# A residual stack of four conditioned layers on one core: feature order in SBUF, DMA shapes and the order of the loading phase

## The chip, the cores and the metric

The kernel runs on one core of one Trainium2 chip. The metric is the device time of one launch in microseconds (us).

## The reference

Four layers, each added to its input x (32 sequences of 128 steps with 512 features): a modulated linear layer, a tanh recurrence, a low-rank layer whose factors come from a small network on the condition, and an LSTM.

```python
x = x + (x * ys) @ weight * rsqrt((ys * ys) @ (weight * weight) + 1e-8)   # ys = cond / sqrt(512)
h = tanh(h @ Wh + x @ Wx + b);  x = x + all h                             # h starts from cond
ae = layernorm(cond) * ln_g + ln_b
xw = gelu(ae @ w1 + b1) @ w2 + b2            # w2: 512 x 8192, xw split into x_a, x_b (512 x 8 each)
x = x + (x + x @ (base + x_a x_b^T))
x = x + LSTM(x; Wx, Wh, b), h0 = cond, c0 = 0     # gates i, f, o, g of 512
```

## The kernel before

All data lie features by tokens: 512 features are 128 partitions times KC = 4 chunks. Work runs in 32 tiles of 4 time steps times 32 sequences (128 columns). Every weight matrix is split into two fp16 parts, high (on ACT, `high`, L477) and low (on DVE, `low`, L756), after its scale is known, and three of the four products of parts are summed on PE.

In the kernel before, feature 4p + c lies in partition p, chunk c. `by_row` loads a square weight that way with four rows, one run of 8 KB, per partition (L350). A tile of x (L354), cond (L613), the bias b1 (L375) and an output tile (L412) are moved with four DMAs each, in runs of 512 B, 128 B and 4 B (x and outputs 512 B, cond 128 B, b1 4 B). On PE a block of 128 output features is every fourth column of a weight (`columns`). The LSTM's gate weights (wx3, wh3) are laid out on the host by chunk and then by gate, and each matmul of `gates_x` (L1378) and `gates_h` (L1386) reads 512 columns in one run; four of them, for four strips of 32 array columns, run at a time.

**The loading phase.** Each engine's order is written out by hand. SP issues the loads in a fixed order: w0, x tile 0, wx1, wh1, w1, four 1 MB blocks of w2 into a ring of four slots (L360), x tiles 1 to 3, b1, wx3 (4 MB), w2 blocks 4 to 7, wh3 (4 MB, into slots freed by w0, wx1 and wh1), base, w2 blocks 8 to 15, b3 (L401), x tiles 4 and 5. Block n of w2 waits until PE's `w2_unit(n - 4)` has used the slot (`w2_used`). ACT issues cond and the layer norm's rows; DVE waits for these four DMAs together (`ld_rows`, 64) before the layer norm (L1070 to L1082), whose output starts PE's work (L1413). Between that and `gates_x(0)` PE runs two or three tiles of the first layers (`l0`, `l1`, `rnn`), 16 units of w2 (L1288), `turn_a`, `z(0)`, `x3_base(0)`, and after the last unit `move_b` (L1309) and `x3_low_rank(0)`. ACT takes squares of each weight for its scale (L480), makes the high parts and the recurrence's tanh (L592); DVE makes the low parts and sums; POOL spreads maxima over partitions (L430). `gates_x(0)` needs x3, so the b factors: `b_magnitude(3)`, `b_scale`, `b_high`, `b_low`, `x3_low_rank(0)`, `low_rank_share(0)`, `x3(0)` (L1001), `x3_high(0)` and the low part of x3.

**The loop** has 30 rounds of four LSTM steps, with a tile of the earlier layers between them, and ends with eight LSTM steps alone (two tiles of output).

## Time and profile before

| | us |
|---|---|
| median of 3 runs | 1192.1 (1191.29 to 1196.86) |
| the profiled execution | 1191.93 |
| its span, first to last instruction | 1190.1 |
| gates_x(0) starts, in the span | 107.16 |
| first lstm step starts | 114.86 |
| last output DMA is issued | 1187.6 |

The span is what the views below cut up; 1.83 us lie outside it. PE is busy for 95% of it.

### The profile page before, as it was taken

What the parts mean: (1) busy time and instruction counts of PE and PEld (TensorE: products, weight loads), DVE (VectorE), ACT (ScalarE), POOL (GpSimd) and SP (SyncE); (2) the same over time, 40 slices, a digit from 0 to 9 for tenths busy, and PEclk for the clock granted to TensorE, in tenths of its full rate; (3) what the DMA queues carried; (4) which work ended last, traced back from release to release, by engine and by line L of the source; (5) the groups of instructions that cost most, each with busy time, mean ns of one, the idle gap of its engine ahead of it and who ended that gap; (6) DMA issues with size and microseconds to landing.
All of it is one profiled execution on the core that took longest, in us unless ns stands there. A gap on an engine that the chain in (4) does not pass through costs nothing.

```text
span 1190.1 us, 50661 instructions
## 1 busy us (share of the span) xinstructions
PE 1133.2 (95%) x22740; PEld 756.6 (64%) x22740; DVE 911.4 (77%) x2645; ACT 425.3 (36%) x1032; POOL 56.2 (5%) x75
## 2 busy tenths in 40 slices
PE   2886999999999999999999999999999999999896
PEld 1653676667666766676677667766776677667542
DVE  4896777787777787877877778777787787777665
ACT  4794333333333332333333323333333233333221
POOL 1000000000000000000000000000000000000000
PEclk9987999999999999999999999999999999999998
DMA  9991000000000000000000000000000000000000
GB/s 323 388 347 42 3 21 20 21 20 21 20 13 10 21 21 21 20 21 20 12 12 21 20 20 21 21 21 11 13 20 21 20 21 21 11 10 5 12 11 19
DMA packets 49065, 51.00 MB, mean 43 GB/s; under 512 B 5984, under 2 KB 38752, under 8 KB 47184
## 3 DMA queue, kind: packets, MB, share of 16 engines
q1 hardware_dynamic: 47984, 47.50, 12.8%
q8 instruction: 178, 2.92, 1.0%
q10 hardware_dynamic: 864, 0.26, 0.1%
q14 instruction: 39, 0.32, 0.1%
HBM read 39.36 MB, written 8.39 MB: 40 GB/s over the span
## 4 chain that ended last, share of the span: by engine, by line
PE 90%; DVE 4%; ACT 2%; DMA 2%; issue 1%; ACTq 0%; DVEq 0%
PE ps_gates L1386 28%; PE ps_gates L1378 27%; PE ps_l L1317 14%; PE ps_x L1317 7%; PE ps_rnn L1402 6%; PE ps_rnn L1405 4%; PE ps_z L1317 2%; PE ps_lr L1317 2%; DMA ring<-in_hw 1%; PE ps_gates L1288 1%; DVE big L756 1%; DMA hb1T_sb<-in_hb1T 1%; ACT wh_hi L477 0%; DVE gates_ring L1012 0%; DVE late L1031 0%
## 5 line engine op out<-in xcount | busy, mean ns | idle before, releaser
L1386 PE MATMUL ps_gates<-big,lstm_h 128*32 128x512 f16 x6144 | 354.4, 379 | 4.4 <-DVE lstm_h L1034 4.4
L1378 PE MATMUL ps_gates<-big,rows 128*32 128x512 f16 x6144 | 345.8, 381 | 3.5 <-DVE rows L756 3.5
L1378 PEld LDWEIGHTS ps_gates<-big,rows 128*32 128x32 f16 x6144 | 165.3, 97 | 172.1 <-issue 6.6
L1386 PEld LDWEIGHTS ps_gates<-big,lstm_h 128*32 128x32 f16 x6144 | 158.1, 97 | 161.7 <-DVE lstm_h L1034 7.3
L599 ACT ACTIVATE gates_ring<-gates_ring 128x256 f32<-128x256 f32 x128 | 53.4, 418 | 337.9 <-DVE gates_ring L1012 337.9
L1012 DVE SCALAR_TENSOR_TENSOR gates_ring<-ps_gates,tile_un,rows 128x256 f32<-128x256 f32 x256 | 111.8, 477 | 68.3 <-PE ps_gates L1386 67.1
L1402 PE MATMUL ps_rnn<-rnn_h,wh_hi 128*128 128x64 f16 x2048 | 120.3, 192 | 6.9 <-DVE rnn_h L855 6.9
L1405 PE MATMUL ps_rnn<-rnn_h,wh_lo 128*128 128x32 f16 x2048 | 116.3, 177 | 0.0
L1402 PEld LDWEIGHTS ps_rnn<-rnn_h,wh_hi 128*128 128x128 f16 x2048 | 93.0, 96 | 35.3 <-issue 27.2
L1031 DVE SCALAR_TENSOR_TENSOR late<-gates_ring,tile_g,cell_tanh 128x128 f16<-128x128 f32 x128 | 45.0, 352 | 60.8 <-ACT cell_tanh L606 60.8
L1405 PEld LDWEIGHTS ps_rnn<-rnn_h,wh_lo 128*128 128x128 f16 x2048 | 91.2, 97 | 0.0
L1317 PE MATMUL ps_l<-xs,w_hi 128*128 128x128 f16 x1024 | 79.7, 222 | 2.1 <-DVE xs L756 1.9
L1317 PE MATMUL ps_l<-x,wx_hi 128*128 128x128 f16 x1024 | 79.3, 221 | 0.4 <-DVE x L756 0.4
L1317 PE MATMUL ps_x<-x,base_hi 128*128 128x128 f16 x1024 | 78.3, 219 | 0.0
L1317 PEld LDWEIGHTS ps_l<-xs,w_hi 128*128 128x128 f16 x1024 | 65.0, 114 | 3.2 <-DVE xs L756 2.0
L1317 PEld LDWEIGHTS ps_l<-x,wx_hi 128*128 128x128 f16 x1024 | 64.7, 114 | 1.4 <-issue 0.8
L1317 PEld LDWEIGHTS ps_x<-x,base_hi 128*128 128x128 f16 x1024 | 63.8, 114 | 0.4 <-issue 0.4
L592 ACT ACTIVATE x_ring<-rnn_pre 128x128 f32<-128x128 f32 x128 | 39.6, 310 | 64.6 <-DVE rnn_pre L849 64.6
L1037 DVE STREAM_TRANSPOSE lstm_hT<-lstm_h 128x128 f32<-128x128 f32 x128 | 53.5, 418 | 4.4
L477 ACT ACTIVATE x<-x_ring,tile_s 128x512 f16<-128x512 f32 x32 | 23.1, 722 | 84.8 <-DVE x_ring L860 84.8
L477 ACT ACTIVATE rnn_h<-x_ring,scales 128x128 f16<-128x128 f32 x128 | 51.5, 402 | 4.2
L606 ACT ACTIVATE cell_tanh<-cell 128x128 f32<-128x128 f32 x128 | 39.8, 311 | 33.0 <-DVE cell L1022 33.0
(181 smaller groups left out, 1560.2 us busy)
## 6 DMA issues: line engine op xcount, KB each, us to landing
ring<-in_hw SPq DMA_DIRECT2D x16, 1024.0 KB, 13.4
xT_sb<-in_xT SPq DMA_DIRECT2D x128, 64.0 KB, 2.4
outT<-late SPq DMA_DIRECT2D x128, 64.0 KB, 2.1
big<-in_wx SPq DMA_DIRECT2D x5, 1024.0 KB, 7.9
big<-in_wh SPq DMA_DIRECT2D x5, 1024.0 KB, 13.4
big<-in_w SPq DMA_DIRECT2D x1, 1024.0 KB, 5.8
big<-in_hw SPq DMA_DIRECT2D x1, 1024.0 KB, 11.8
late<-in_base SPq DMA_DIRECT2D x1, 1024.0 KB, 19.5
```

The source lines that it names most:

```text
L477: return nc.scalar.activation(out_, in_, ACT.Copy, scale=scale)
L592: nc.scalar.activation(h, rnn_pre[:], ACT.Tanh).then_inc(rnn_h_ready, 1)
L599: nc.scalar.activation(gates[:, 0:2 * P], gates[:, 0:2 * P], ACT.Sigmoid).then_inc(gates_acted, 1)
L606: nc.scalar.activation(cell_tanh[:], cell[:], ACT.Tanh).then_inc(cell_tanh_ready, 1)
L1012: nc.vector.scalar_tensor_tensor(gates[:, half], ps_gates[t % 2][:, half], tile_un[:, a, 0:1], b3_sb[:, half], ALU.mult, ALU.add).then_inc ...
L1031: nc.vector.scalar_tensor_tensor(lstm_hs, gates[:, 2 * P:3 * P], tile_g[:, following, 1:2], cell_tanh[:], ALU.mult, ALU.mult).then_inc(lst ...
L1037: nc.vector.transpose(lstm_hT[:], columns(lstm_h[:])).then_inc(lstm_hT_ready, 1)
L1317: last = nc.tensor.matmul(psum, w, x, start=(n == 0), stop=(n == len(triples) - 1))
L1378: nc.tensor.matmul(ps_gates[t % 2][B * j:B * j + B, :], x16[:, part, k, at:at + B], wx3_part(w_part, k)[:, GW * j:GW * j + GW], start=(n = ...
L1386: last = nc.tensor.matmul(ps_gates[t % 2][B * j:B * j + B, :], lstm_h16[:, part, k], wh3_part(w_part, k)[:, GW * j:GW * j + GW], start=Fal ...
L1402: nc.tensor.matmul(ps_rnn[:, at:at + 2 * B], wh1_hi[:, k, P * oc:P * oc + P], rnn_h16[:, k].rearrange("p h b -> p (h b)"), start=(k == 0), ...
L1405: last = nc.tensor.matmul(ps_rnn[:, at:at + B], wh1_lo[:, k, P * oc:P * oc + P], rnn_h16[:, k, 0], start=False, stop=(k == KC - 1))
```

## The change

Feature 128k + p now lies in partition p, chunk k, for all tensors. A tile of x, an output tile, cond and b1 are one DMA each, with 2 KB, 2 KB, 512 B and 16 B per partition; square weights come in four runs of 2 KB per partition. On PE and DVE blocks of features are contiguous. The gate matmuls read their 512 columns as 16 runs of 32, and the gates lie in PSUM by gate, chunk and column; b3 is loaded in that order with 16 DMAs of 128 B runs. cond is SP's first load, the layer norm's rows are ACT's, and hb1 has a semaphore of its own. base is loaded ahead of wh3. `x3` is cut into `x3_first` and `x3_low`; `rnn` on ACT into `rnn_tanh` and `rnn_high`. The orders of all five engines up to the loop are written anew; the parts of them not shown move the same calls (squares, high and low parts, tanh steps) to other places. The loop's order is as before.

```diff
         def by_row(w):
-            return w.rearrange("(p k) n -> p k n", k=KC)
-
-
-        def by_block(x, j):
-            return x.rearrange("(f k) j n -> j f k n", k=KC)[j]
-
-        def columns(x):
-            return x.rearrange("p (q c) -> p c q", c=KC)
-
-
-        def loaded_columns(w, oc):
-            return w.rearrange("p (k q c) -> p k q c", k=KC, c=KC)[:, :, :, oc]
+            return w.rearrange("(k p) n -> p k n", k=KC)
+
+
+
+        def tile_columns(w, j):
+            return w.rearrange("p (k g j q) -> p j g k q", k=KC, g=GATES, q=B)[:, j]
+
+        def by_gate(x):
+            return x.rearrange("p (g k q) -> p g k q", g=GATES, q=B)
+
+        def by_chunk(x):
+            return x.rearrange("p (k q) -> p k q", q=B)
...
             def load_x(c):
-                for j in range(KC):
-                    sp.dma_start(xT_sb[c % XT_RING][FB * j:FB * j + FB].rearrange("p k t b -> p k (t b)"),
-                                 by_block(xT[c].rearrange("p j t b -> p j (t b)"), j)).then_inc(ld_x[c % XT_RING], 16)
+                sp.dma_start(xT_sb[c % XT_RING][:].rearrange("p k t b -> p (k t b)"),
+                             xT[c].rearrange("p j t b -> p (j t b)")).then_inc(ld_x[c % XT_RING], 16)
...
+            sp.dma_start(condT_sb[:], condT).then_inc(ld_cond, 16)
             load_weight(w0, W0_SLOT, ld_w0)
...
-            for j in range(KC):
-                sp.dma_start(b1T_sb[FB * j:FB * j + FB], b1T.rearrange("(f k) j -> j f k", k=KC)[j],
-                             allow_slow_non_contiguous=True).then_inc(ld_b1, 16)
+            sp.dma_start(b1T_sb[:], b1T).then_inc(ld_b1, 16)
...
             for n in range(RING, 2 * RING):
                 sp.wait_ge(w2_used, n - RING + 1)
                 load_w2(n)
+            sp.dma_start(late[:].rearrange("p (k n) -> p k n", k=KC), by_row(base)).then_inc(ld_base, 16)
...
-                sp.dma_start(b3_sb[B * j:B * j + B], b3[j].partition_broadcast(B)).then_inc(ld_b3, 16)
+                for g in range(GATES):
+                    sp.dma_start(by_gate(b3_sb[B * j:B * j + B])[:, g],
+                                 b3.rearrange("k (g j q) -> g j k q", g=GATES, q=B)[g, j].partition_broadcast(B)).then_inc(ld_b3, 16)
             sp.wait_ge(x1_ready, 1)
...
-                for j in range(KC):
-                    sp.dma_start(by_block(out[a].rearrange("p j t b -> p j (t b)"), j),
-                                 x3T[a % 2][FB * j:FB * j + FB].rearrange("p k t b -> p k (t b)"))\
-                      .then_inc(st_out[a % 2], 16)
+                sp.dma_start(out[a].rearrange("p j t b -> p (j t b)"),
+                             x3T[a % 2].rearrange("p k t b -> p (k t b)")).then_inc(st_out[a % 2], 16)
...
-            def wh1_low(oc):
-                dve.wait_ge(wh1_hi_ready, oc + 1)
-                low(wh1_lo[:, :, P * oc:P * oc + P], loaded_columns(big[:, WH1_SLOT], oc), s_wh1,
-                    wh1_hi[:, :, P * oc:P * oc + P]).then_inc(wh1_lo_ready, 1)
+            def wh1_low(k):
+                dve.wait_ge(wh1_hi_ready, k + 1)
+                low(wh1_lo[:, k], loaded(big[:, WH1_SLOT])[:, k], s_wh1, wh1_hi[:, k]).then_inc(wh1_lo_ready, 1)
...
-            for j in range(KC):
-                act.dma_start(condT_sb[FB * j:FB * j + FB], by_block(condT, j)).then_inc(ld_cond, 16)
             act.dma_start(ln_rows[:, 0], cond).then_inc(ld_rows, 16)
             act.dma_start(ln_rows[:, 1], ln_g.partition_broadcast(B)).then_inc(ld_rows, 16)
             act.dma_start(ln_rows[:, 2], ln_b.partition_broadcast(B)).then_inc(ld_rows, 16)
-            act.dma_start(hb1T_sb[:], hb1T).then_inc(ld_rows, 16)
-
+            act.dma_start(hb1T_sb[:], hb1T).then_inc(ld_hb1, 16)
+
+
+            act.wait_ge(consts_ready, 1)
+            nc.scalar.activation(unused[:], cell[:, 0:1], ACT.Sqrt)
+            act.wait_ge(ld_w0, 16)
+            squares(big[:, SQ_SLOT], big[:, W0_SLOT], 1)
             act.wait_ge(ln_var_ready, 1)
             nc.scalar.activation(ln_s[:, 1:2], ln_s[:, 0:1], ACT.Sqrt).then_inc(ln_root_ready, 1)
-            act.wait_ge(ld_w0, 16)
-            squares(big[:, SQ_SLOT], big[:, W0_SLOT], 1)
             act.wait_ge(ld_wx1, 16)
             unused_squares(big[:, WX1_SLOT], 2, 1)
+            act.wait_ge(dsum_parts, 1)
+            nc.scalar.activation(folded, ps_x3[:], ACT.Copy).then_inc(dsum_moved, 1)
+            w0_high(0)
             act.wait_ge(aeT_ps, 1)
             nc.scalar.activation(aeT, ps_z[:, 0:P].rearrange("p (k b) -> p k b", b=B), ACT.Copy).then_inc(aeT_ready, 1)
-            act.wait_ge(dsum_parts, 1)
-            nc.scalar.activation(folded, ps_x3[:], ACT.Copy).then_inc(dsum_moved, 1)
-            act.wait_ge(ld_wh1, 16)
-            unused_squares(big[:, WH1_SLOT], 3, 2)
-            w0_high(0)
             xs_high(0)
             w0_high(1)
+            wx1_high(0)
...
             wh3_high(1, 1)
+            copy_rows(3)
+            rnn_tanh(7)
+            b_high()
             wh3_high(2, 0)
-            copy_rows(3)
             wh3_high(2, 1)
+            low_rank_share(0)
+            x3_high(0)
             wh3_high(3, 0)
-
-            nc.scalar.activation(unused[:], s_h, ACT.Sigmoid)
-            b_high()
+            wh3_high(3, 1)
+            rnn_high(7)
...
-            dve.wait_ge(ld_rows, 64)
+            dve.wait_ge(ld_rows, 48)
             linked(nc.vector.bn_stats(stats, ln_rows[:, 0]))
             linked(nc.vector.bn_aggr(moments, stats))
             nc.vector.tensor_scalar(ln_s[:, 0:1], moments[:, 1:2], LN_EPS, None, ALU.add).then_inc(ln_var_ready, 1)
             x_magnitude(0, 0)
+            xs(0)
...
             b_magnitude(3)
-            wh3_low(2, 0)
+            wh3_low(1, 0)
             b_scale()
             x3_bound()
             gate_scales(0)
             b_low()
+            wh3_low(1, 1)
+            wh3_low(2, 0)
+            x3_first(0)
             wh3_low(2, 1)
-            dve.wait_ge(lstm_hi_ready, 1)
-            low(lstm_h16[:, 1], condT_sb[:], tile_g[:, 0, 1:2], lstm_h16[:, 0]).then_inc(lstm_lo_ready, 1)
+            x3_low(0)
             wh3_low(3, 0)
-            x3(0)
             wh3_low(3, 1)
             rnn_out(7)
             x2(1)
+            dve.wait_ge(lstm_hi_ready, 1)
+            low(lstm_h16[:, 1], condT_sb[:], tile_g[:, 0, 1:2], lstm_h16[:, 0]).then_inc(lstm_lo_ready, 1)
             x2_low(1)
...
-                            nc.tensor.matmul(ps_gates[t % 2][B * j:B * j + B, :], x16[:, part, k, at:at + B],
-                                             wx3_part(w_part, k)[:, GW * j:GW * j + GW], start=(n == 0 and k == 0), stop=False,
+                            nc.tensor.matmul(by_gate(ps_gates[t % 2][B * j:B * j + B, :]), x16[:, part, k, at:at + B],
+                                             tile_columns(wx3_part(w_part, k), j), start=(n == 0 and k == 0), stop=False,
                                              tile_position=(0, B * j))
...
             pe.wait_ge(folds_ready, 3)
-            pe.wait_ge(ae_ready, 1)
-            for k in range(KC):
-                last = nc.tensor.transpose(ps_z[:, B * k:B * k + B], columns(ae)[:, k], ident[0:B, 0:B])
-            last.then_inc(aeT_ps, 1)
             pe.wait_ge(ys_ready, 2)
             pe.wait_ge(sq_ready, 1)
             folded_parts(ps_x3, ysq, w0_sq).then_inc(dsum_parts, 1)
+            pe.wait_ge(ae_ready, 1)
+            for k in range(KC):
+                last = nc.tensor.transpose(ps_z[:, B * k:B * k + B], ae[:, P * k:P * k + P], ident[0:B, 0:B])
+            last.then_inc(aeT_ps, 1)
...
+            w2_unit(3)
             pe.wait_ge(wx1_lo_ready, 2)
             l1(0)
-            w2_unit(3)
+            l0(1)
             pe.wait_ge(wh1_lo_ready, KC)
             pe.wait_ge(h0_lo, 1)
             rnn(0)
-            l0(1)
+            w2_unit(4)
             rnn(1)
-            w2_unit(4)
             w2_unit(5)
+            w2_unit(6)
             rnn(2)
+            w2_unit(7)
             l1(1)
+            turn_a()
             rnn(3)
-            w2_unit(6)
-            w2_unit(7)
             l0(2)
-            turn_a()
             rnn(4)
-            rnn(5)
-            l1(2)
             w2_unit(8)
             w2_unit(9)
+            rnn(5)
             w2_unit(10)
-            w2_unit(11)
             pe.wait_ge(a_lo_ready, 4)
             z(0)
+            w2_unit(11)
+            l1(2)
             rnn(6)
+            w2_unit(12)
+            w2_unit(13)
+            rnn(7)
+            w2_unit(14)
+            w2_unit(15)
+            move_b()
             pe.wait_ge(base_lo_ready, 2)
             x3_base(0, range(KC))
-            w2_unit(12)
-            w2_unit(13)
-            w2_unit(14)
-            rnn(7)
-            w2_unit(15)
-            move_b()
             pe.wait_ge(b_lo_ready, 2)
```

## Rows read from the trace of the kernel before

**Rows 1.** Windows of the loading phase and of the loop: us, busy us per engine, PEclk, DMA, GB/s.
```profile
14.67:107.16 92.49, 66.48 (x852) 42.65 (x853) 78.55 (x186) 72.23 (x97) 8.31 (x12) 0.90 0.87 306
120.00:1130.00 1010.00, 1006.96 (x20820) 682.98 (x20821) 789.80 (x2329) 335.42 (x888) 47.05 (x56) 1.00 0.07 17
```

**Rows 2.** The chain of waits in order of time, from the start to 130 us: start us, us, what.
```profile
5.07 9.57 DMA hb1T_sb<-in_hb1T
...
18.43 0.69 DVE rows L1082
...
80.62 13.07 DMA ring<-in_hw
...
98.58 1.28 ACT L693
...
103.47 1.01 DVE big L756
...
104.67 0.75 DVE late L1001
...
106.26 0.77 DVE rows L756
...
107.16 7.88 PE ps_gates L1378 x96
...
118.59 0.71 PE ps_z L1317 x24
...
121.98 1.34 PE ps_x L1317 x24
...
126.89 5.18 PE ps_gates L1378 x96
```

**Rows 3.** Windows: the last two columns are the DMA engines' busy share and GB/s.
```profile
44.00:50.00 6.00, 4.12 (x79) 3.09 (x77) 3.56 (x12) 3.80 (x7) 0.00 (x0) 1.00 1.03 379
55.00:65.00 10.00, 10.00 (x186) 8.52 (x184) 9.79 (x15) 9.45 (x13) 0.00 (x0) 1.00 1.00 412
75.50:80.50 5.00, 5.00 (x51) 1.44 (x48) 4.60 (x15) 4.65 (x7) 0.32 (x1) 1.00 0.40 118
91.00:93.00 2.00, 0.66 (x25) 0.56 (x21) 1.27 (x3) 0.26 (x1) 0.00 (x0) 1.00 1.22 217
```

**Rows 4.** DMA view of 27 to 31 us: packets and bytes in it.
```profile
DMA packets 2166, 0.86 MB, mean 215 GB/s; under 512 B 747, under 2 KB 2146, under 8 KB 2150
```

**Rows 5.** Timeline of PE: start us, us, line, operation, tiles [idle before <-releaser].
```profile
64.96 0.28 PE L1402 MATMUL ps_rnn<-rnn_h,wh_hi 128*128 128x64 f16 x4
...
76.92 3.64 PE L1288 MATMUL ps_gates<-ring,lstm_h 128*32 128x512 f32 x32
...
89.63 1.07 PE L1288 MATMUL ps_gates<-ring,lstm_h 128*32 128x512 f32 x8 [1.86 <-DMA ring<-in_hw]
...
93.74 1.07 PE L1288 MATMUL ps_gates<-ring,lstm_h 128*32 128x512 f32 x8 [2.08 <-DMA ring<-in_hw]
95.52 3.46 PE L1309 MATMUL ps_l<-rows,half_ident 128*64 128x512 f32 x8 [0.72 <-ACT rows L543]
```

**Rows 6.** Timeline of SP: the issues of b3.
```profile
81.11 2.81 SPq L401 DMA_DIRECT2D rows<-in_b  x4
```

**Rows 7.** Timeline of ACT: its first activation.
```profile
15.76 0.20 ACT L620 ACTIVATE rows<-rows 32x1 f32<-32x1 f32 x1 [8.93 <-DVE rows L1072]
```

**Rows 8.** Low parts on DVE from 15 to 107 us, by line: busy us, mean ns.
```profile
L756 DVE SCALAR_TENSOR_TENSOR big<-big,l_scales 128x1024 f16<-128x1024 f32 x16 | 20.4, 1278 | 0.5 <-issue 0.3
L756 DVE SCALAR_TENSOR_TENSOR wh_lo<-big,scales,wh_hi 128x512 f16<-128x512 f32 x4 | 4.5, 1138 | 0.0
```

**Rows 9.** Timeline of the end: the last hidden state's transposition, the last tile's issue.
```profile
1184.12 0.31 DVE L1034 STREAM_TRANSPOSE lstm_h<-late 128x128 f16<-128x128 f16 x1
...
1185.73 2.50 SPq L412 DMA_DIRECT2D outT<-late  x4
```

**Rows 10.** The page, part 6: output DMAs, KB each, us from issue to landing.
```profile
outT<-late SPq DMA_DIRECT2D x128, 64.0 KB, 2.1
```

## Prediction before the run

> **What bounds the kernel now.** I read the windows first. In the loop PE is busy for 1006.96 of 1010 us at full clock [rows 1], so nothing there gets faster unless PE has less to do; the change leaves its instructions, their number and their sizes alone. What can give is the part outside: 107.16 us until `gates_x(0)` starts [rows 2], and the end.
>
> In the loading phase three things are near their limit. DVE is busy for 78.55 of 92.49 us, ACT for 72.23 [rows 1]. The DMA engines are at or above a busy share of 1.00 in most windows at 379 to 412 GB/s, but not from 75.5 to 80.5 us, where the share is 0.40 and the rate 118 [rows 3]. The chain of waits says which ends last. It starts with hb1T's landing at 14.64 (5.07 + 9.57), although the layer norm needs nothing of hb1; it crosses the long wait for a w2 block (issued at 80.62, 13.07 us), and from the last block runs through the b factors to `gates_x(0)` [rows 2]. So the question is when the last w2 block lands, now 93.74 us, and what follows it, now 107.16 - 93.74 = 13.42 us [rows 2, 5].
>
> The stretch without DMA work has its cause on PE: units 8 to 11 of w2 run at 76.92, 3.64 us for 32 matmuls, behind `rnn(5)` and `l1(2)` [rows 5]. Their ring slots come free only then, and everything loaded earlier has run out.
>
> **The change part by part.** Sums are made against the profiled execution, 1191.93 us, which is 0.17 below the median of the runs. The times of the loading phase are in the span.
>
> *Small packets.* From 27 to 31 us, when x tiles 1 to 3 and b1 are moved, 2166 packets carry 0.86 MB at 215 GB/s [rows 4]: 4 us x 16 engines / 2166 = 29.5 ns for one, and 91 to 93 us, with x tiles alone, run at the same 217 [rows 3]. Before, three tiles are 3 x 512 packets of 512 B and b1 512 of 4 B: 2048 x 29.5 ns / 16 = 3.8 us. After, the tiles go in 2 KB like w2, 0.79 MB at 379 GB/s = 2.1 us, and b1 is 128 packets, 0.2 us: 1.5 us less. x tile 0 and cond were 1024 packets, 1.9 us; now 0.26 MB at 379 and 128 packets, 0.9: 1.0 less. Together -2.5 us.
>
> The Trainium skill (DMA: Bandwidth & Descriptors, "Specifications") has 512 B as the smallest transfer that reaches line rate. The rows disagree: 512 B pieces ran at 217 against 379 for 2 KB. By the rule the x tiles would give nothing; that is rival C.
>
> *Larger pieces lost.* Five square weights of 1 MB go from 8 KB to 2 KB runs. wh3 and base, in 8 KB, ran at 412, w2 in 2 KB at 379 [rows 3]; 5.24 MB x (1/379 - 1/412) = 1.1 us at most, and none at least, since the other loads share those windows. I take +0.5.
>
> *The stretch without work.* In the new order units 8 and 9 come right after `rnn(4)`, unit 10 after `rnn(5)`, unit 11 after `z(0)`. Each slot then is refilled as its block has landed and been used, with two or three blocks still queued. Filling it gives 5 us x (1 - 118/395) = 3.5 us, at a rate midway between 379 and 412. This holds only if PE reaches unit 8 before the queue runs dry, so if `rnn(4)` is done by about 68 us. It should be: the layer norm waits for three DMAs that are issued 2.8 us earlier (cond's four issues are gone from ACT) and not for hb1, so `ae`, at 19.12 now (18.43 + 0.69 [rows 2]), comes about 5 us earlier; and ACT, idle for 8.93 us until 15.76 behind the layer norm's root [rows 7], takes w0's squares as soon as w0 is there. With 5 to 6 us of lead all through, `rnn(4)` (64.96 now [rows 5]) falls near 60. DVE also saves on wh1: 1138 ns for 512 elements with a stride of four [rows 8], against about 0.75 for the same operation without one (the low part of x3, 0.77 [rows 2]): 4 x 0.38 = 1.5 us. Cover for all of it is the DMA stream; if that is not the bound, this lead is worth its own size (rival A).
>
> *b3.* 16 DMAs of 128 pieces of 128 B: 2048 x 29.5 / 16 = 3.8 us of DMA work in place of 128 pieces of 2 KB (0.7), and 16 issues of 0.70 us (2.81 / 4 [rows 6]) = 11 us on SP in place of 2.8. SP has nothing urgent behind them: x tiles 4 and 5 are needed only in the loop, and `lstm_sums(0)`, the first reader, comes over 20 us later. But b3 is queued just behind block 15. Now the gap between blocks 14 and 15 is 93.74 - 89.63 = 4.11 us [rows 5], where 1.05 MB at 379 take 2.8: 1.3 us go to what is queued behind (b3 and two x tiles, 0.7 + 1.9 us of work). After, that work is 3.8 + 1.4 = 5.2. Bounds: 0 (in order) and +2.6 (twice the work, all of it shared and more); I take +0.7.
>
> Last landing: 93.74 - 2.5 + 0.5 - 3.5 + 0.7 = 88.9, **-4.8 us**.
>
> *Behind the last block.* Kept on the old clock, block 15 at 93.74: `move_b` still runs from 95.52 for 3.46 us, to 98.98 [rows 5]. `x3_base(0)` now follows it instead of lying in the wait before: 2 x 1.34 = 2.7 us [rows 2], to 101.7. The b chain on ACT loses its table load (98.58, 1.28 us [rows 2]), done earlier, so `b_low` ends at about 100.6 and x3_base is what ends last before the low-rank product (24 matmuls of 64 columns, 0.71 as for z [rows 2]): 102.4. `low_rank_share` is an ACT operation on the 512 columns that `x3_high` has, 0.84 with its waits (104.67 + 0.75 to 106.26 [rows 2]): 103.3. `x3_first` does not wait for a low part of wh3 as now (103.47 to 104.48, then 104.67 [rows 2]): 103.3 to 104.1. `x3_high` to 104.9, but DVE is in `wh3_low(2, 1)`, 1.28 us [rows 8], to 105.3, and `x3_low`, 0.77 [rows 2], ends at 106.1. `gates_x(0)` at 106.2 instead of 107.16: **-1.0 us**. If PE's clock should be down in this stretch, x3_base is up to 2.7 longer and the term turns to +1.7. The last two low parts of wh3, now behind x3_low, have 2.6 us against `gates_x(0)`'s share of 7.88 for 96 matmuls [rows 2]: hidden. That stretch runs at a lower clock now (5.18 for 96 in the loop [rows 2]) because PE stood idle before it; it will again, so 0, with -2.7 as the end of the range.
>
> *The loop.* Gate matmuls read 16 runs of 32 instead of one of 512, four at a time. No row shows that. Nearest: z reads runs of 16, 24 matmuls in 0.71 us [rows 2] = 29.6 ns against 26.7 for 64 columns at 2.4 GHz, and the base product with whole runs has 1.34 / 24 = 55.8 against 53.3 [rows 2]. The extra is the same per matmul, not per run, so 0. The high end: all of z's extra 2.9 ns is its four runs, 0.7 each, 16 of them cost 11.6 against the gates' present 216 - 213 = 3 ns (5.18 / 24 [rows 2]): +8.6 ns for each of 3072 groups of four, +26 us. No low end, since 216 ns is already the columns. The other blocks' stationary operands lose a stride, at a spacing of 55.8 that the 128 columns set: 0. The transposition of the hidden state (0.31 us [rows 9]) reads without a stride and is on the path only in the last eight steps: within 0.1 each, +-0.8; 0 taken, as nothing shows it stride-bound.
>
> *The end.* The last tile's four issues take 2.50 us [rows 9], landing 2.1 after the last [rows 10]. One issue saves 3 x 0.62 = 1.9 and moves 192 KB more in one DMA, 0.5 at 379: **-1.4 us**, bounds -0.6 and -1.9.
>
> Sum: -4.8 - 1.0 - 1.4 = -7.2, so **1184.7 us**.
>
> **The rivals.** About 0.5% (6.0 us) is what a measurement tells from no change: faster means below 1186.1, slower above 1198.1.
>
> A. *DVE and ACT become the bound.* For: 14 us idle of 92 on DVE is little slack, and orders written by hand leave holes (the DVE idle of the new order is unknown). With a start 5.4 earlier, 1.5 less work and 4 us more idle, `gates_x(0)` comes at 107.16 - 2.9 = 104.3; with the end, 1187.6. Against: the new start fills holes rather than making them. 0.27.
>
> B. *Slower: the gate matmuls' runs.* For: four streams at a time from neighbouring addresses, which z does not test. From +4.3 ns in 216 per group (13.2 us / 3072) the kernel is slower by over 0.5%; at the high end above, 1184.7 + 26 = 1211. Against: z, and the same bytes read. 0.08. The Trainium skill (SBUF — State Buffer, "Door 1: The DMA port swizzle", note on cachelines) has full bandwidth for a line of 16 B hit at least twice; runs of 64 B fill such lines, which speaks against B, and no run shows it for four streams.
>
> C. *Packet size does not matter* (the rule above; the slow stretches would be b1's tiny pieces and latency). The 2.5 us are gone: 1187.2. Against: 217 GB/s at 91 to 93 us, without b1. 0.05.
>
> D. *Nothing moves*: b3's pieces delay block 15 by the full 3.8 + 1.4 and the DMA stretch reappears elsewhere, since unit 10 or 11 waits for `rnn(5)` or a's low parts. 1191.93 - 2.5 + 0.5 + 2.6 - 1.0 - 1.4 = 1190.1. 0.04.
>
> **How the numbers follow.** The forecast has 0.56. Its own range is 1180.8 (no cost of b3 or of 2 KB runs, and `gates_x(0)` at full clock) to 1187.5. Down to 1181 and up to 1190.5 takes in A, C and D, and leaves out B and a little at each side. Faster than 1186.1: 0.57, from the forecast's cases less those above 1186, with a few of A's below; same 0.34; slower 0.09.
>
> **What would show it.** Right: DMA share near 1 without a stretch like 75.5 to 80.5, last w2 block near 89, `gates_x(0)` near 101.5, 96 gate matmuls in 5.18 us as before, a single output issue at the end. Wrong: idle PE before an `rnn` step rather than before w2 (A); 96 gate matmuls in more than 5.3 us (B); x tiles still at 217 GB/s (C); block 15 over 4 us behind block 14 (b3's price).

## The result, and the profile after

Six runs of the changed kernel took 1181.64 us in the median (1180.78 to 1182.61), six of the kernel before 1191.45 (1189.69 to 1196.86): ratio 0.9905, 95% interval 0.9884 to 0.9926. Against the 1192.1 us of the first three runs that is 1180.8. The forecast was 1184.7, 1181.0 to 1190.5: the direction was right and the gain was larger, at or just beyond the range's low end.

The profiled execution after took 1180.78 us, the lowest of the six, its span is 1179.0 against 1190.1; so the traces lie 11.1 us apart and the medians 9.8. PE's timeline, to be read beside [rows 5]:

```profile
67.21 1.94 PE L1294 MATMUL ps_gates<-ring,lstm_h 128*32 128x512 f32 x8 [3.82 <-DMA ring<-in_hw]
...
84.48 1.07 PE L1294 MATMUL ps_gates<-ring,lstm_h 128*32 128x512 f32 x8
...
86.56 1.07 PE L1294 MATMUL ps_gates<-ring,lstm_h 128*32 128x512 f32 x8 [1.01 <-DMA ring<-in_hw]
88.34 1.94 PE L1315 MATMUL ps_l<-rows,half_ident 128*64 128x512 f32 x8 [0.72 <-ACT rows L539]
...
100.02 6.71 PE L1384 MATMUL ps_gates<-big,rows 128*32 128x512 f16 x96 [5.33 <-DVE rows L759]
106.55 2.77 PE L1392 MATMUL ps_gates<-big,lstm_h 128*32 128x512 f16 x48
...
1169.46 2.77 PE L1392 MATMUL ps_gates<-big,lstm_h 128*32 128x512 f16 x48 [0.56 <-DVE lstm_h L1035]
```

The last line of it is the last LSTM step; in the kernel before that step is here:

```profile
1178.57 2.77 PE L1386 MATMUL ps_gates<-big,lstm_h 128*32 128x512 f16 x48 [0.56 <-DVE lstm_h L1034]
```

PE's unit for the last w2 block, block 15, starts at 86.56 instead of 93.74 (-7.18), `gates_x(0)` at 100.02 instead of 107.16 (-7.14), the first LSTM step at 106.55 instead of 114.86. The last step's lead is 9.11 us, the span's 11.1. So the distance is -7.14 up to `gates_x(0)`, -1.17 in it and `gates_x(1)`, -0.80 in the loop, -2.0 behind the start of the last step. Unit 8 now waits for its block and not the block for it.

The windows after, against [rows 3] (columns as in [rows 1]), show no stretch without DMA work up to 85 us:

```profile
core 0: us, PE busy (x) PEld busy (x) DVE busy (x) ACT busy (x) POOL busy (x), PEclk, DMA share, GB/s
70.00:75.00 5.00, 5.00 (x48) 1.68 (x48) 2.05 (x4) 3.26 (x7) 0.38 (x1) 0.50 1.05 387
75.00:80.00 5.00, 5.00 (x95) 4.08 (x92) 3.47 (x15) 2.93 (x4) 0.00 (x0) 0.95 1.05 387
80.00:85.00 5.00, 5.00 (x92) 2.30 (x88) 4.12 (x7) 3.13 (x6) 0.00 (x0) 1.00 1.07 346
85.00:90.00 5.00, 3.27 (x24) 0.64 (x16) 4.18 (x7) 2.85 (x4) 0.90 (x1) 1.00 0.61 150
```

SP's timeline is where the rest of it can be read: tiles 1 to 3 are issued in 4.03 us, and tiles 4 and 5 only at 87.22, behind the sixteen issues of b3.

```profile
16.02 4.03 SPq L351 DMA_DIRECT2D xT_sb<-in_xT  x3
20.09 0.64 SPq L372 DMA_DIRECT2D b1T_sb<-in_b1T  x1
...
77.64 9.54 SPq L398 DMA_DIRECT2D rows<-in_b  x16
87.22 0.90 SPq L351 DMA_DIRECT2D xT_sb<-in_xT  x2
```

DVE's and GpSimd's timelines ahead of `gates_x(0)`: `x3_low(0)` (98.11) takes 1.76 us, not the 0.77 of [rows 2], and GpSimd's xs(3), which started 0.98 us before it, still runs.

```profile
93.68 2.66 DVE L759 SCALAR_TENSOR_TENSOR big<-big,l_scales 128x1024 f16<-128x1024 f32 x2
96.26 0.74 DVE L1000 SCALAR_TENSOR_TENSOR late<-ps_x,tile_un,rows 128x512 f32<-128x512 f32 x1
96.92 1.27 DVE L759 SCALAR_TENSOR_TENSOR big<-big,l_scales 128x1024 f16<-128x1024 f32 x1
98.11 1.76 DVE L759 SCALAR_TENSOR_TENSOR rows<-late,tile_g,rows 128x512 f16<-128x512 f32 x1
...
97.13 2.19 POOL L436 TENSOR_TENSOR xsT<-xT_sb,ysT 128x512 f32<-128x512 f32 x1 [6.70 <-issue]
```

The end on SP's timeline after, against [rows 9]:

```profile
1176.53 0.33 SPq L409 DMA_DIRECT2D outT<-late  x1
```

And the page's part 6 after, against [rows 10]:

```profile
outT<-late SPq DMA_DIRECT2D x32, 256.0 KB, 2.0
```

### The profile page after: what moved, and what is told of

It is laid out like the page before. It is cut to its first block, busy times and chain, and to the rows that moved or that the text cites. A ratio compares the mean times of both kernels' runs of the same rounds, so it can differ in the third digit from the quotient of the medians.

```text
span 1179.0 us, 50475 instructions
## 1 busy us (share of the span) xinstructions
PE 1131.5 (96%) x22740; PEld 752.7 (64%) x22740; DVE 894.3 (76%) x2645; ACT 423.4 (36%) x1033; POOL 55.8 (5%) x75
## 4 chain that ended last, share of the span: by engine, by line
PE 89%; DVE 3%; DMA 2%; ACT 2%; issue 2%; SPq 1%; POOL 0%; DVEq 0%; ACTq 0%; POOLq 0%
PE ps_gates L1392 28%; PE ps_gates L1384 27%; PE ps_l L1323 14%; PE ps_x L1323 7%; PE ps_rnn L1408 6%; PE ps_rnn L1411 4%; PE ps_z L1323 2%; PE ps_lr L1323 2%; DMA late<-in_base 1%; DMA big<-in_hw 1%; ACT gates_ring L476 1%; SPq L357 1%; PE ps_gates L1294 0%; DVE gates_ring L1013 0%; DVE late L1032 0%
## 5 line engine op out<-in xcount | busy, mean ns | idle before, releaser
L1323 PEld LDWEIGHTS ps_l<-x,wx_hi 128*128 128x128 f16 x1024 | 61.7, 98 | 4.9 <-issue 4.9
L1323 PEld LDWEIGHTS ps_x<-x,base_hi 128*128 128x128 f16 x1024 | 61.4, 98 | 1.2 <-issue 1.2
L1050 DVE SCALAR_TENSOR_TENSOR lstm_h<-lstm_hT,tile_g,lstm_h 128x128 f16<-128x128 f32 x128 | 44.6, 348 | 9.6 <-DVE lstm_hT L1038 3.2
L848 DVE SCALAR_TENSOR_TENSOR rnn_half<-ps_rnn,un_rnn,xw1T 128x128 f32<-128x128 f32 x128 | 44.5, 347 | 9.5 <-PE ps_rnn L1411 5.5
```

What stands on the lines that cost most here:

```text
L848: nc.vector.scalar_tensor_tensor(rnn_half[:], sums[:, :, 1], un_rnn[:], xw1T[:, :, s], ALU.mult, ALU.add).then_inc(rnn_half_ready, 1)
L1050: nc.vector.scalar_tensor_tensor(lstm_h16[:, 1], lstm_hT[:], tile_g[:, following, 1:2], lstm_h16[:, 0], ALU.mult, ALU.subtract).then_inc(l ...
L1323: last = nc.tensor.matmul(psum, w, x, start=(n == 0), stop=(n == len(triples) - 1))
```

## The experiments

Each row of this table is one kernel: the group of runs that it was measured in, and the median of its runs; from its trace, the start of w2's block 15, how long PE waited for it, how long `move_b` then took, from block 15's start to that of `gates_x(0)`, and the length of the 96 matmuls of `gates_x(0)` and (1).

| kernel | group | us | block 15 | waited | move_b | to gates_x(0) | gates_x |
|---|---|---|---|---|---|---|---|
| before | 0 | 1191.45 | 93.74 | 2.08 | 3.46 | 13.42 | 7.88 |
| after | 0 | 1181.64 | 86.56 | 1.01 | 1.94 | 13.46 | 6.71 |
| order_only | A | 1190.19 | 91.75 | 2.42 | 3.68 | 14.52 | 6.94 |
| layout_only | A | 1183.26 | 89.35 | 0.99 | 1.94 | 13.42 | 7.16 |
| b3_whole | A | 1182.50 | 86.75 | 2.11 | 3.68 | 14.26 | 7.05 |
| x3_low_first | A | 1181.74 | 86.32 | 1.32 | 3.63 | 12.32 | 4.32 + 2.77 |
| x_in_512 | B | 1181.94 | 87.52 | 1.82 | 3.68 | 14.75 | 6.69 |
| x_in_32p | C | 1183.66 | 88.85 | 2.13 | 1.94 | 12.44 | 7.35 |
| x_in_32p_b3_whole | C | 1187.11 | 90.80 | 2.83 | 3.68 | 14.67 | 8.12 |
| b1_in_4b | C | 1181.87 | 86.94 | 0.84 | 1.94 | 13.46 | 6.83 |
| units_late | B | 1187.25 | 90.85 | 3.02 | 3.68 | 14.60 | 8.09 |
| x_in_32p_b3_units | D | 1190.79 | 94.77 | 3.61 | 3.68 | 14.77 | 8.23 |
| pool_after_x3 | B | 1180.87 | 86.97 | 1.73 | 3.38 | 12.44 | 8.28 |
| clock_kept | C | 1180.61 | 87.18 | 1.62 | 3.42 | 13.38 | 5.36 |
| behind_shorter | D | 1180.22 | 86.55 | 0.71 | 1.94 | 11.55 | 7.94 |
| behind_and_clock | D | 1178.91 | 86.60 | 1.69 | 1.94 | 11.46 | 5.36 |
| out_in_four | B | 1183.25 | 86.92 | 1.57 | 1.94 | 13.46 | 7.69 |

Kernels that leave the x tiles and PE's order as in the changed kernel, pieces of 512 B apart, have block 15 between 86.3 and 87.2 us: a difference under 0.9 us in that column says nothing. The same holds for the last column: after, b1_in_4b and out_in_four, which do the same there and wait for it equally long (5.32 or 5.33 us), have 6.71, 6.83 and 7.69.

The groups A to D were run on four different chips. The kernel before was run again in each, with medians of 1193.3, 1191.92, 1193.6 and 1191.38 us; the changed kernel was run in group 0 alone. So where a text below sets a median of A to D against the changed kernel's 1181.64, a difference of 1 us or so is not shown by it; medians within a group are the better comparison.

**The change in two halves.** order_only has the new orders of all engines on the old layout and the old DMAs; layout_only the new feature order, the new shapes of the DMAs and the new blocks, with the old orders:

```diff
 order_only, of the old shapes:
-                sp.dma_start(xT_sb[c % XT_RING][:]...
+                for j in range(KC):
+                    sp.dma_start(xT_sb[c % XT_RING][FB * j:FB * j + FB]...
 layout_only, of the old orders:
-            w2_unit(8)
-            w2_unit(9)
             rnn(5)
...
+            w2_unit(8)
+            w2_unit(9)
```

> The changed kernel with the old feature order, DMA shapes and strided blocks, the orders new. Theory 1: last w2 block 3.5 us earlier than before through the stretch that is filled, gates_x(0) near 103.5, loop and end as before: 1188. Theory 2: gates_x(0) near 100, 1184.5.

> The kernel before with the new feature order, DMA shapes and contiguous blocks, all engines' orders as they were. If the loads' shapes carry the gain in the loading phase (theory 1), the last w2 block lands 2 us earlier, but the stretch without DMA work at 76 to 80 us stays, because PE's order makes it: gates_x(0) at 104.5 to 105.5, loop 0.6 shorter, end 2.0 shorter, 1187 us. If the orders carry all of it (theory 2), only loop and end change: 1189.5.

Measured: order_only 1190.19 us, ratio to before 0.9979 (0.9964 to 0.9993); layout_only 1183.26, ratio 0.9911 (0.9885 to 0.9936). Neither theory had it: the layout alone brings most of the gain, the orders alone about 0.2%. The windows of 5 us say why. order_only fills the stretch of 75 to 80 us (387 GB/s), worth 3.6 us, but up to 75 us it has moved 26.69 MB where the kernel before had 27.29, worth 1.6; the 2.0 that are left are its lead at block 15. layout_only keeps a weaker stretch (279 and 319 GB/s from 70 to 80 us, 2.3 us lost in place of 3.6), since PE comes to units 8 to 11 earlier. PE in layout_only, the four units in one piece and block 15:

```profile
73.18 3.82 PE L1279 MATMUL ps_gates<-ring,lstm_h 128*32 128x512 f32 x32
...
89.35 1.06 PE L1279 MATMUL ps_gates<-ring,lstm_h 128*32 128x512 f32 x8 [0.99 <-DMA ring<-in_hw]
```

SP's timeline in order_only, the three x tiles as 12 DMAs:

```profile
17.16 10.81 SPq L351 DMA_DIRECT2D xT_sb<-in_xT  x12
```

The same tiles as 3 DMAs on SP's timeline in layout_only:

```profile
16.70 3.87 SPq L351 DMA_DIRECT2D xT_sb<-in_xT  x3
```

**b3's pieces, and DVE's order.** Two single edits of the changed kernel: b3 laid out on the host and loaded in four DMAs; and `x3_low(0)` ahead of `wh3_low(2, 1)`.

```diff
-                for g in range(GATES):
-                    sp.dma_start(by_gate(b3_sb[B * j:B * j + B])[:, g], ...)
+                sp.dma_start(b3_sb[B * j:B * j + B], b3[j].partition_broadcast(B)).then_inc(ld_b3, 16)
```
```diff
             x3_first(0)
-            wh3_low(2, 1)
             x3_low(0)
+            wh3_low(2, 1)
```

> The changed kernel with b3 laid out on the host in the new order, so that four DMAs with 2 KB pieces load it. If b3's 2048 small pieces delay block 15, as the prediction had it, the last block comes 0.7 to 2 us earlier and the time falls as much. If SP's slow issuing (9.5 us for 16) keeps them out of block 15's way, the last block stays at 86.6 or comes later, since b3 and x tiles 4 and 5 then crowd in behind it as before: time equal or up to 1 us more.

> The changed kernel with x3_low(0) on DVE ahead of wh3_low(2, 1). If the low part of wh3 in front of it and the slow execution beside POOL's xs (1.69 us for 0.75) are what took back the 1.0 us expected behind the last block, x3_low ends 1.2 us earlier or more and gates_x(0) starts at 98.0 to 98.8: 1180.3. If gates_x(0) then waits for the parts of wh3 instead, nothing moves.

Measured: 1182.5 (1180.79 to 1184.07) and 1181.74 (1180.21 to 1181.92). b3's 2048 pieces of 128 B cost the last block nothing that can be told (86.75 against 86.56). In b3_whole x tiles 4 and 5 are issued at 79.47, right behind block 15, and they do not delay it either. x3_low_first has `gates_x(0)` 1.1 us closer to block 15 although move_b was 1.7 us longer, but then the low parts of wh3 held `gates_x(1)`; no gain is left in the median.

**What made the x tiles slow: pieces or partitions.** x_in_512 moves each tile in four DMAs of 512 B pieces over all 128 partitions, x_in_32p in four DMAs of 2 KB pieces over 32 partitions each. Before, a DMA had both, 32 partitions and 512 B. A tile is four DMAs of 64 KB in all three, so what four DMAs cost in place of one is in each figure.

```diff
+                for j in range(KC):
+                    sp.dma_start(xT_sb[c % XT_RING][:, j]...                  (x_in_512)
+                    sp.dma_start(xT_sb[c % XT_RING][FB * j:FB * j + FB]...    (x_in_32p)
```

> The changed kernel with each x tile moved in four DMAs of 512 B pieces again (only that part of the old shapes is back; b1, cond and the order stay new). Theory 1, the smaller number of pieces is what brought the last w2 block forward: the window 20 to 40 us falls from 403 GB/s to about 365, SP's issues of tiles 1 to 3 take 8 us or more instead of 4.0, block 15 lands 2.3 to 3.5 us later (89 to 90 instead of 86.6), time 1184 to 1185. Theory 2, pieces of 512 B cost what pieces of 2 KB cost, and the order brought it: block 15 within 0.5 us of 86.6, time 1181.6.

> The changed kernel with each x tile moved in four DMAs of 32 partitions each, in pieces of 2 KB. With pieces of 512 B over all 128 partitions the tiles had cost next to nothing (20 to 40 us at 390 GB/s against 403). Theory 1, what ran at half rate before was the set of 32 partitions that one DMA wrote, whatever the size of its pieces: about 217 GB/s while tiles 1 to 3 are moved, SP's issues of them take 9 us or more instead of 4.0, block 15 1.5 to 2.5 us later (88 to 89), time 1183.5. Theory 2, it takes short pieces and few partitions together: the tiles run at 390, time 1181.6.

Windows of 1 us in x_in_512 (columns: us, PE busy, PEclk, DMA share, GB/s):

```profile
27.00:28.00 1.00, 1.00 (x12) 1.00 1.17 323
28.00:29.00 1.00, 1.00 (x16) 1.00 1.29 305
29.00:30.00 1.00, 1.00 (x16) 1.00 1.22 327
```

The same windows in x_in_32p:

```profile
28.00:29.00 1.00, 1.00 (x16) 1.00 1.07 246
29.00:30.00 1.00, 1.00 (x16) 1.00 1.14 277
```

x_in_512 comes near its theory 2 (block 15 1.0 us late, not within 0.5), x_in_32p fits theory 1 in block and time. Both matter, and the partitions more. Against the rate of the changed kernel in each us from 26 to 33 (377 to 442 GB/s), x_in_512 falls short by some 0.30 MB, x_in_32p by 0.66, and the kernel before by 0.99: at 388 GB/s 0.8, 1.7 and 2.5 us. The two parts add up to the whole (0.96 of 0.99 MB). x_in_32p is the only one of them that moves the time (+2.0 us against the changed kernel, +1.8 against b1_in_4b of its own group; x_in_512 +0.3, within the spread). The Trainium skill (SBUF — State Buffer, "Door 1: The DMA port swizzle") has a range of 32 partitions reach 8 of the 16 ports, at half the bandwidth of 128: the 215 to 217 GB/s of [rows 3, 4] are such a half; x_in_32p has 246 to 316 from 27 to 32 us, with other loads in the same windows, which fits but does not show the half by itself. Its rule of 512 B for line rate (DMA: Bandwidth & Descriptors, "Specifications"), which the prediction weighed, is off by a fifth here (305 to 327 against 389 to 409 in the changed kernel) and not by the 217 against 379 that the prediction held against it.

**b1 in pieces of 4 B.**

```diff
+            for j in range(KC):
+                sp.dma_start(b1T_sb[FB * j:FB * j + FB], b1T.rearrange("k p -> p k")[FB * j:FB * j + FB], ...)
```

> The changed kernel with b1 in four DMAs of 32 partitions and pieces of 4 B again (512 pieces), all else new. Theory 1, b1 was part of the slow stretch: 512 pieces at 29.5 ns on 16 engines are 0.9 us, block 15 0.5 to 1.0 us later, time 1182.3. Theory 2, it costs nothing: 1181.6.

Theory 2, as far as can be told. Measured 1181.87 us (1181.33 to 1185.04), block 15 at 86.94.

**Slow tiles beside the last block.**

> As the run before, and b3 in four DMAs instead of sixteen, so that SP comes to x tiles 4 and 5 at about 80 us, before the last w2 block has landed, as in the kernel before, and not at 87. Theory 1, the two tiles in DMAs of 32 partitions slow the last block when they are queued beside it: block 15 another 1.0 to 1.5 us later (89 to 90.5), time 1184.5; the sixteen issues of b3 then were a shield for the last block. Theory 2, a block that is queued ahead isn't slowed by what is queued behind it: block 15 as in the run before.

The edit is that of x_in_32p with that of b3_whole. Measured 1187.11 us (1186.3 to 1187.86), 3.45 more than x_in_32p of the same group, and more than theory 1 had. SP comes to tiles 4 and 5 at 82.99, and PE then stands waiting for block 15:

```profile
86.91 1.07 PE L1293 MATMUL ps_gates<-ring,lstm_h 128*32 128x512 f32 x8
...
90.80 1.94 PE L1293 MATMUL ps_gates<-ring,lstm_h 128*32 128x512 f32 x8 [2.83 <-DMA ring<-in_hw]
93.45 3.68 PE L1314 MATMUL ps_l<-rows,half_ident 128*64 128x512 f32 x8 [0.72 <-ACT rows L538]
```

The same two units in x_in_32p:

```profile
85.65 1.07 PE L1295 MATMUL ps_gates<-ring,lstm_h 128*32 128x512 f32 x8
...
88.85 1.07 PE L1295 MATMUL ps_gates<-ring,lstm_h 128*32 128x512 f32 x8 [2.13 <-DMA ring<-in_hw]
```

Block 15 is 3.89 us behind block 14 instead of 3.20, and the wait has a second price: unit 15 and `move_b` run at half the rate (1.94 and 3.68 us, not 1.07 and 1.94). So some 0.7 us of the distance is the gap itself and 2.2 what comes behind the block (14.67 against 12.44): the slower clock, and 1.0 from `x3_low`, of which more below. The other 1.25 us stand already at unit 8 (70.33 against 69.08), ahead of anything that b3's DMAs could touch; these two traces are of the lowest run of x_in_32p and the highest of this kernel, so a part of their distance is spread. The 3.45 us of the medians stand; what the traces show of their cause for certain is the 0.7 and what follows from a longer wait.

**The stretch without work, put back.**

```diff
             rnn(4)
+            rnn(5)
+            l1(2)
             w2_unit(8)
             w2_unit(9)
-            rnn(5)
             w2_unit(10)
+            w2_unit(11)
             pe.wait_ge(a_lo_ready, 4)
             z(0)
-            w2_unit(11)
-            l1(2)
```

> The changed kernel with w2 units 8 to 11 again behind rnn(5) and l1(2) on TensorE. Theory 1, the filled stretch is worth the 3.5 us of the prediction beside the new shapes too: a stretch with a DMA share under 0.5 appears ahead of 80 us, block 15 near 90, time 1185. Theory 2, the stretch is worth what the run with the new layout and the old orders lost in it (1.6 us of idle DMA engines between 70 and 80 us): block 15 near 88.2, time 1183.2. Theory 3, the DMA engines are ahead of the need anyway: 1181.6.

Measured 1187.25 us (1186.66 to 1187.62), beyond theory 1: +5.6. Its windows:

```profile
70.00:75.00 5.00, 5.00 (x54) 4.23 (x52) 3.70 (x5) 4.78 (x8) 1.10 (x1) 0.65 0.76 281
75.00:80.00 5.00, 4.62 (x60) 1.69 (x56) 0.34 (x2) 1.12 (x2) 0.00 (x0) 1.00 0.49 163
```

(106 + 224) GB/s x 5 us are 1.65 MB not moved, 4.3 us at 387, and block 15 is 4.3 us later. Behind the block it is another 1.1 us (14.60 against 13.46), where `move_b` runs at half the rate after a wait of 3.02 us instead of 1.01. `gates_x` is 1.4 us longer, but its idle time ahead is shorter than in the changed kernel (4.68 against 5.33), and kernels alike differ by 1.0 there; that part is not the landing's.

**All three together.**

> The changed kernel with three of its parts undone together: x tiles in DMAs of 32 partitions, b3 in four DMAs (so tiles 4 and 5 queued beside the last blocks), units 8 to 11 behind rnn(5) and l1(2). Theory 1, these three are the whole of the earlier landing and add up: block 15 near 94 (90.8 with the first two, 4.3 more by the units), time 1191 to 1193. Theory 2, they overlap, since a DMA stretch without work lets the slow tiles catch up: block 15 near 91, time 1188.

Measured 1190.79 us (1189.4 to 1191.99) beside 1191.38 for the kernel before: ratio 0.9991 (0.9976 to 1.0005). Block 15 at 94.77: theory 1, though the time is just under its range. Three parts of the change, put back, take away all of the gain: the partitions of the x tiles, their place beside the last block, PE's order of the units. Singly they cost 2.0, 3.45 and 5.6 us, 11.1 together; here it is 9.2, so they overlap a little. The gains of the loop and of the end are still in this kernel: its first LSTM step comes 2.7 us later than in the kernel before (117.59 against 114.86). In the loading phase the rest of the change by itself is a loss.

**Behind the last block.** pool_after_x3 holds GpSimd's xs(3) until x3_low(0) is done; clock_kept adds 16 groups of four matmuls, whose sums are overwritten; behind_shorter and behind_and_clock are candidates for a better kernel.

```diff
 pool_after_x3
+            pool.wait_ge(x3_lo_ready, 1)
             xs(LAG + 1)
 clock_kept (behind_and_clock: 8 groups)
             pe.wait_ge(wx3_lo_ready, 2 * KC)
+            for n in range(16):
+                for j in range(KC):
+                    nc.tensor.matmul(by_gate(ps_gates[0][B * j:B * j + B, :]), b_hi[:, 0, 0:B],
+                                     tile_columns(wx3_part(0, 0), j), start=True, stop=True, ...)
             gates_x(0)
 behind_shorter, beside pool_after_x3's edit
-            wh3_low(2, 0)
             x3_first(0)
-            wh3_low(2, 1)
             x3_low(0)
+            wh3_low(2, 0)
+            wh3_low(2, 1)
...
-            pe.wait_ge(wh3_lo_ready, 2 * KC)
             gates_x(1)
+            pe.wait_ge(wh3_lo_ready, 2 * KC)
```

> The changed kernel with GpSimd's xs(3), a tensor operation of 2.2 us that runs beside DVE's x3_low(0), held back until x3_low(0) is done. Theory 1, DVE's x3_low took 1.76 us and not 0.75 because GpSimd runs beside it: it falls to about 0.75, gates_x(0) starts 1.0 us earlier (99.0), time 1180.6. Theory 2, DVE's operation is slow by itself (its operands lie otherwise now): still 1.7 us and 1181.6 us.

> The changed kernel with 64 more matmuls (16 groups of four, 512 columns; their sums are overwritten) on TensorE in the idle time between the low-rank product of b and gates_x(0), some 3.5 us at full clock. Theory 1, TensorE's granted clock is down in gates_x(0) and gates_x(1) because it stood idle for 5.3 us before them: they take 5.3 us instead of 6.7, time 1180.2. Theory 2, the clock falls whatever stands there: same stretch, and the added matmuls at half clock delay gates_x(0) by 1.5 us or more, 1183.

> The changed kernel with DVE going from b_low and wh3_low(1, 1) straight to x3_first(0) and x3_low(0), the five other low parts of wh3 behind them, GpSimd's xs(3) held until x3_low(0) is done, and TensorE's wait for wh3's low parts moved behind gates_x(1), which doesn't read them. Theory 1, DVE's order is what ends last ahead of gates_x(0): it starts 11.4 us behind block 15 instead of 13.5; but the five low parts (1.28 us each) end about 6.5 us later and hold lstm(0) if gates_x(0) and (1) take 5.3 to 7 us, so of 2.1 us some 1 to 1.5 are left: time 1180.3. Theory 2, the low parts turn into the new wait for all of it: 1181.6 or later.

> As behind_shorter, with 32 added matmuls (8 groups of four, 1.7 us at full clock) ahead of gates_x(0). Theory 1, clock and DVE's order are separate costs and add up: gates_x(0) 11.5 us behind block 15 and 5.3 us long with gates_x(1), time 1179.0. Theory 2, at full clock the matmuls are done before the low parts of wh3 and lstm(0) waits for those: no better than the added matmuls alone, 1180.6.

In pool_after_x3 `x3_low(0)` takes 0.74 us, and `gates_x(0)` comes 12.44 us behind block 15 instead of 13.46:

```profile
98.53 0.74 DVE L760 SCALAR_TENSOR_TENSOR rows<-late,tile_g,rows 128x512 f16<-128x512 f32 x1
```

The Trainium skill (SBUF — State Buffer, "Who interferes with whom") has a VectorE instruction with two inputs in SBUF contend with a GpSimd instruction that reads SBUF; 1.76 against 0.74 us agrees. The two only have to start in the other order: in the eight traces with 1.75 to 1.77 us xs(3) started 0.07 to 1.09 us before `x3_low(0)`, in x_in_32p 0.07 us behind it (100.47 against 100.40), and there `x3_low(0)` took 0.74. The median is 1180.87 us (1180.16 to 1181.76), 0.8 under the changed kernel's, which is within the spread of either; in the trace `gates_x` took 8.28 us and ate the gain.

Windows of PE alone in the changed kernel (columns as for x_in_512):

```profile
96.00:98.00 2.00, 0.00 (x0) 0.50 0.00 0
98.00:100.00 2.00, 0.00 (x0) 0.50 0.00 0
100.00:102.00 2.00, 1.98 (x20) 0.50 0.03 8
```

The same windows in clock_kept:

```profile
96.00:98.00 2.00, 2.00 (x44) 1.00 0.03 8
98.00:100.00 2.00, 1.43 (x28) 1.00 0.00 0
100.00:102.00 2.00, 1.44 (x28) 1.00 0.00 0
```

PE idle for 5.33 us has its granted clock at 0.50, 1.2 GHz, when `gates_x(0)` starts; with the added matmuls it stays at 1.00, and the 96 matmuls take 5.36 us instead of 6.71. The median is 1180.61 us (1180.0 to 1181.05), all runs under the lowest of b1_in_4b in the same group (1181.33).

behind_shorter measured 1180.22 us (1179.95 to 1180.48), as its theory 1 had it; `gates_x(0)` comes 11.55 us behind block 15, and `gates_x` takes 7.94, most of it at half clock. behind_and_clock has both; PE:

```profile
98.06 5.36 PE L1385 MATMUL ps_gates<-big,rows 128*32 128x512 f16 x96 [1.48 <-DVE rows L760]
104.07 2.77 PE L1393 MATMUL ps_gates<-big,lstm_h 128*32 128x512 f16 x48 [0.64 <-DVE big L760]
```

1178.91 us (1178.33 to 1179.32), theory 1 again. That is 1.3 us under behind_shorter in the same group, with no overlap of the runs: the price of the clock in this place. Against the changed kernel it is less sure: all runs are under its lowest (1180.78), but they are of another group, and the ratio to before, 0.9902 (0.9885 to 0.9918, where before went from 1189.46 to 1197.17), does not differ from the changed kernel's 0.9905. By the medians it is the fastest version found. The low parts of wh3 have become the wait, 0.64 us, so what stands behind the last block is near its end in this order.

**The output in four DMAs.**

```diff
+                for j in range(KC):
+                    sp.dma_start(out[a][FB * j:FB * j + FB]..., x3T[a % 2][FB * j:FB * j + FB]...)
```

> The changed kernel with each output tile stored in four DMAs of 32 partitions. Theory 1, the 2.0 us that the end is shorter by come from the number of issues behind the last step: the last tile's issues take 2.2 to 2.5 us instead of 0.33, time 1183.5. Theory 2, they come from the shorter transposition and the shape of the output in memory: 1181.9.

Measured 1183.25 us (1183.13 to 1183.28), +1.6, near the time of theory 1. But only a part of that is the output. From the first issue of the last tile to the end of the span it is 3.42 us, 2.47 in the changed kernel and 4.37 in the kernel before: four DMAs give back 0.95 of 1.90. The rest of this trace's distance stands ahead of the first LSTM step, mostly in `gates_x` (7.69). The four issues take 1.71 us in the place of 0.33, where [rows 9] had 2.50:

```profile
1177.88 1.71 SPq L410 DMA_DIRECT2D outT<-late  x4
```

## Why the prediction fell short

Most of it held: the sign, the place (the last w2 block's landing), the stretch that the new order fills, and no price in the gate matmuls. The step of the prediction that failed is the one on **what is queued behind block 15**, with the term of +0.7: it is 1.9 of the 3.9 us that the forecast lacked. Of the rest, 1.2 is the clock in `gates_x`, 0.8 the loop, 0.6 the end and 0.5 the larger pieces, less 1.0 that did not come behind the last block.

*Small packets, -2.5.* Right in size by luck, wrong in mechanism. Up to 75 us the changed kernel has moved 28.24 MB and the kernel before 27.29 (sums of the windows): 0.95 MB, 2.4 us at 388 GB/s. All of it is from 25 to 35 us, with x tiles 1 to 3, where the text had 1.5; of the 1.0 for x tile 0 and cond nothing is seen, up to 25 us both have moved the same. And the 29.5 ns for a packet were taken for a price of small pieces. The runs show 512 B over 128 partitions to cost a third of it and DMAs that write 32 partitions two thirds, with pieces of 2 KB; b1's 4 B pieces nothing that can be told. Rival C was refuted, since the layout does give the time, but half of its reasoning stands: 512 B alone is worth only 0.8 us.

*Larger pieces lost, +0.5.* Not seen: the windows from 40 to 60 us run at 400 GB/s after and 395 before. It is in the 2.4 above.

*The stretch, -3.5.* Measured in the windows of 75 to 80 us, 387 GB/s instead of 110: 1.39 MB, 3.6 us. units_late confirms cause and price (4.3 us at block 15). `rnn(4)` came at 61.4, 3.6 us earlier than before and not 5 to 6, still ahead of the 68 us that mattered. And the new orders without this move are a loss: units_late is 4.0 us slower than layout_only, which keeps the old orders throughout.

*Behind block 15, +0.7.* Measured -1.2: the -7.18 less the 2.4 and the 3.6, a remainder. The text saw that block 15 lost 1.3 us to what is queued behind it. It took this for a price on the amount of that work, which grows from 2.6 to 5.2 us with b3's small pieces, and added 0.7. The loss went away instead. b3_whole shows that b3's pieces cost the block nothing. What the runs show to cost it is x tiles 4 and 5 as DMAs of 32 partitions, issued beside the last blocks (at 84 us before, with 217 GB/s from 91 to 93 us [rows 3]): block 15 comes 0.7 us later behind block 14 in x_in_32p_b3_whole than in x_in_32p, and 0.6 later in x_in_32p_b3_units than in units_late (4.68 against 4.08). That is about half of the 1.2; the other half no run separates (b3's own DMAs write 32 partitions in every kernel). In the changed kernel these tiles write all partitions, and they go out at 87.22, behind b3's sixteen issues, the 9.54 us on SP that the prediction rated as harmless. Either is enough: with tiles of the old partitions the issues are a shield (x_in_32p against x_in_32p_b3_whole), with the new tiles b3_whole does without it.

*Behind the last block, -1.0.* Measured +0.04, and the forecast's steps were right up to the last. x3_first started 9.70 us behind block 15 where the steps give 9.56, and `x3_low` is the whole miss: 1.76 instead of 0.77, beside GpSimd's xs. Where xs starts behind it (pool_after_x3, x_in_32p) the distance is 12.44, forecast 12.46. The text allowed for a low clock in x3_base (+2.7); it was real, but a step earlier: move_b took 1.94 or 3.68 us, the longer in the four runs with the longest waits for block 15, and in some others.

*`gates_x` at a lower clock, 0 with -2.7.* -1.17, most of it luck: clock_kept shows that the low clock comes from PE's idle time, but how long it lasts differs between executions (6.71 us in this trace, 7.69 in out_in_four with the same idle time, 7.88 before).

*The loop, 0.* Rival B fell: 96 gate matmuls take 5.18 us as before. The loop gives 0.80 us all the same, and it comes with the layout: from the first LSTM step to the last it is 1063.71 us before and 1063.73 in order_only, 1062.91 after and in layout_only. 0.58 of it grow evenly, 0.02 us in each of the first 29 rounds. The load of a weight of the square blocks takes 98 ns where it took 114 (order_only 114, layout_only 98); the same matmuls hardly differ (219 ns), and no run takes this part of the layout alone, so the cause is open.

*The end, -1.4 with -1.9.* -2.0: 1.9 from the last tile's issue to the end of the span and 0.1 in the last step, where the transposition of the float32 state takes 0.31 us instead of 0.40. out_in_four gives back half of the 1.9 (0.95); it keeps 2 KB pieces, so the other half goes with the old pieces of 512 B and the old feature order (order_only has 4.47 us, the kernel before 4.37), which were not tried alone.

Sum by the traces: -7.18 + 0.04 - 1.17 - 0.80 - 2.0 = -11.1, against -7.2; the medians have -9.8, since the trace after is of the lowest run and that of before of one 0.5 us above the median. Rivals A and D do not fit either: units 8, 9 and 15 wait for the DMAs, not PE for DVE or ACT, and the stretch did not come back.

## What to carry to other kernels

When a window runs at half the DMA rate, look at which partitions its DMAs write as well as at the size of the pieces, and test the two apart; and ask of each slow transfer what else is on the queue beside it, the last transfer that the path waits for above all. A part that is late is dearer than its lateness where an engine's clock falls while it waits: here 4.3 us at the landing were 5.6 in the time. And what a set of new orders gives does not show what its parts give: all orders together are worth 1.3 us on the old layout (3.1 against before in order_only's own group) and 1.6 on the new one, yet PE's new place for four units is worth 5.6 us beside the others, which without it are a loss.

## What the runs showed beside that

- SP is held longer by more DMAs of the same bytes: 12 for the same three tiles take 8.0 us (x_in_32p), 10.0 (x_in_512) or 10.8 (order_only), 3 take 4.0. How much of it is the issue and how much a full queue, no run tells.
- A VectorE operation that took 0.74 us takes 1.76 when a GpSimd tensor operation has started just before it. On the path to `gates_x(0)` this is 1 us; in the time of the kernel it could not be told.
- 64 useless matmuls in a gap of 5.3 us let the 96 behind them run at full clock, 5.36 us instead of 6.71; 32 of them made behind_and_clock 1.3 us faster than behind_shorter.
